# Expert stage of a perceiver block: SyncE's requests for page rows are tied to the landing of expert weights, and one request of ScalarE is moved

## The reference

```python
probs = sigmoid(x @ router_w.T + expert_bias)        # 160 experts
top_w, top_idx = top_k(probs, 8)
top_w = 2.5 * top_w / (sum(top_w) + 1e-9)
h1 = silu(einsum('th,eih->eti', x, w_gate))          # 256 -> 128 for each expert
routed = einsum('eti,ehi->th', h1 * combine.T, w_down)   # 128 -> 256
out = x + routed + silu(x @ w_gate_shared.T) @ w_down_shared.T
```

## Time and profile before

| | |
|---|---|
| median of 3 runs | 1392.87 us (1391.3 to 1392.95) |
| profiled execution, its time | 1392.75 us |
| its span, first to last instruction | 1391.3 us |
| TensorE busy | 1244.5 us (89%) |
| the steps of the expert stage | from 1012.9 us to 1328 us of the span |
| reading back and summing | from 1339 us to the end |

### The profile page before, as it was taken

How to read it: one execution, slowest core, us unless ns; L and a number is a source line. 1 busy time by engine, 2 the same in 40 slices (tenths; PEclk the granted TensorE clock), 3 DMA queues, 4 the chain that set the end, 5 groups by cost and what they waited for, 6 DMA issues and landing times. The chain is left out here.

```text
span 1391.3 us, 34815 instructions
## 1 busy us (share of the span) xinstructions
PE 1244.5 (89%) x11693; PEld 900.0 (65%) x11693; DVE 945.6 (68%) x2728; ACT 604.5 (43%) x1761; POOL 548.3 (39%) x717
## 2 busy tenths in 40 slices
PE   4999999999998589999999999997759999999946
PEld 2667667767766357777767677766537766766725
DVE  2477666666666446787788877877627776767737
ACT  2445555455454156676566676574201111111140
POOL 1011111101100102456566566667506766766730
PEclk8999999999999679999999999999959999999969
DMA  9322323233323000111121111113298988898658
GB/s 290 114 91 96 132 90 140 90 132 107 132 80 106 31 16 16 48 53 56 60 76 56 64 53 61 60 37 110 90 278 245 266 257 259 260 256 252 204 226 349
DMA packets 124881, 185.74 MB, mean 134 GB/s; under 512 B 23286, under 2 KB 90517, under 8 KB 122785
## 3 DMA queue, kind: packets, MB, share of 16 engines
q10 hardware_dynamic: 57696, 77.47, 17.7%
q1 hardware_dynamic: 50880, 71.38, 17.0%
q0 software_dynamic: 16128, 34.67, 7.0%
HBM read 190.88 MB, written 78.25 MB: 193 GB/s over the span
## 5 line engine op out<-in xcount | busy, mean ns | idle before, releaser
L1052 POOL DMA_INDIRECT y_d<-y,xg x208 | 203.7, 979 | 128.9 <-DVE y L1048 92.7
L1022 ACT ACTIVATE ex<-bank 128x256 f32<-128x256 f32 x104 | 39.9, 383 | 286.4 <-PE bank L1017 98.7
L773 POOL DMA_INDIRECT xs_d<-xw,slot_id x128 | 134.7, 1053 | 30.3 <-issue 29.4
L472 ACT ACTIVATE ex<-bank,nmC 128x256 f32<-128x256 f32 x256 | 118.9, 481 | 14.3 <-DVE nmC L466 13.8
L1048 DVE COPY y<-bank 128x512 f32<-128x512 f32 x104 | 71.8, 691 | 75.3 <-PE bank L1042 71.6
L485 PE MATMUL bank<-ident,ex 128*128 128x128 f32 x512 | 79.1, 284 | 19.9 <-ACT ex L472 16.5
L485 PEld LDWEIGHTS bank<-ident,ex 128*128 128x128 f32 x512 | 61.8, 145 | 54.3 <-ACT ex L472 21.0
L466 DVE TENSOR_REDUCE nmC<-bank 128x2 f32<-128x512 f32 x128 | 82.8, 680 | 5.6 <-PE bank L457 4.8
L1006 DVE COPY ex<-bank 128x512 f32<-128x512 f32 x104 | 71.4, 687 | 21.9 <-PE bank L1002 18.2
L1002 PE MATMUL bank<-ident,xg 128*128 128x128 f32 x416 | 70.7, 295 | 16.7 <-DMA xg<-xs_d 16.7
L1316 POOL TENSOR_TENSOR stB<-stB,small 128x1 f32<-128x1 f32 x32 | 20.2, 632 | 165.3 <-DVE stB L1313 165.3
(11 more groups left out here) (390 smaller groups left out, 3317.7 us busy)
## 6 DMA issues: line engine op xcount, KB each, us to landing
xs_d<-zeros ACTq DMA_DIRECT2D x16, 1768.0 KB, 7.4
pTC<-in_wexp ACTq DMA_DIRECT2D x104, 256.0 KB
xg<-xs_d SPq DMA_DIRECT2D x306, 68.0 KB
cT<-in_ctx SPq DMA_DIRECT2D x32, 512.0 KB, 4.1
wh<-in_wexp ACTq DMA_DIRECT2D x52, 256.0 KB
cT<-in_wexp ACTq DMA_DIRECT2D x52, 256.0 KB
kTC<-in_wexp ACTq DMA_DIRECT2D x52, 256.0 KB
vvC<-in_wexp ACTq DMA_DIRECT2D x52, 256.0 KB
```

Of the source, the lines that this page charges most:

```text
L472: last = act.activation(ex[:, u, 256 * b:256 * b + 256], bank[hp][:, 256 * b:256 * b + 256], ACT.Exp, bias=nm[:, u, b:b + 1], accum_out=su ...
L773: pool.indirect_dma_start(out=xs_d, out_offset=bass.IndirectOffsetOnAxis(ap=slot_id[z][:, k:k + 1], axis=0), in_=xw[z][:, k, :], in_offset ...
L1052: pool.indirect_dma_start(out=y_d, out_offset=bass.IndirectOffsetOnAxis(ap=who, axis=0), in_=y[:, n, g, :], in_offset=None, bounds_check=l ...
```

## The change

```
+    GATED = range(2, UNITS)
...
         def rows_sp(m):
+            if m in GATED:
+                d = 2 * (m - 2)
+                sp.wait_ge(s_w[d % RING_W], (d // RING_W + 1) * 64)
             page = load_numbers(nc, mybir.EngineType.SP, table[1], m, 4 if m < EARLY else 8)
             fetch(sp, 2 * m, page, range(4 if m < EARLY else 3))
...
         rows_act(0)
         load(0)
         load(1)
-        for m in range(1, EARLY):
-            rows_act(m)
+        rows_act(1)
         for m in range(UNITS):
             rows_sp(m)
         for i in range(DOUBLES + DOWN):
             if i < RING_W - 2:
                 load(i + 2)
             elif RING_W <= i + 1 < DOUBLES:
                 load(i + 1)
+            if i == 1:
+                rows_act(2)
             if i < DOUBLES:
                 turn(i)
```

## The result

Over 20 runs each the changed kernel takes 1397.76 us in the median and the kernel before 1394.33 us. The ratio is 1.0027, with a 95% interval of 1.0015 to 1.0040: slower by 3.8 us (2.1 to 5.6). The prediction was 1400 us against a median of 1392.87, so slower by 7.1 us, with the rows of the page requests landing last.

The account below looks back on a forecast made before the run. The prediction saw a DMA-bound start and a TensorE-bound long stretch. Its terms, -3 us at the start and +10 us steady, made +7 us: 1400 us, with an 8-in-10 range of 1388 to 1414.

Parts of the forecast that it names:

- What bounds the kernel: Whole expert stage: a start bound by DMAs, then a long stretch bound by TensorE at 2.69 us a step.
- Start, SyncE: -3 us: First eight steps: gates hold back row pages, so weights land sooner; 3 us gained, bounds 0 to 5.4 us.
- the 18 pages: Start: pages not yet requested when weights of double 5 land, 24 in place of 42; 1.25 MB or 4.3 us.
- Start, ScalarE: nothing: Start: loads 2 and 3 requested 3.2 us sooner, load(4) no sooner; no term in the sum.
- Steady stretch: +10 us: Long stretch: gated rows land last; 17 units lose 0.85 us in the mean, 15 us less a third; bounds 0 to 45.
- The room: Steady stretch: time from just-in-time weights at the gate to the `turn` that needs the rows, 4.6 us.
- rival A: Whole kernel: rows become the last to land, slower by 3 to 21 us, 1396 to 1414; chance 0.58.
- B: Gate hidden in the steady stretch and weights profit from held-back rows: faster, 1385 to 1390; chance 0.22.
- C: Both terms small or equal: start -3 us, steady loss 1 to 5 us, 1391 to 1395.7; chance 0.20.
- D: SyncE's gate does nothing because the ring's wait opens later than the gate; chance 0.
- The fit: Steady stretch: 2.0 us plus bytes at 436 GB/s; a page lands in 2.2 us, need 4.2 us, no stall, 1390.

Follow-up runs that it names:

- three gates with the move: Changed kernel with SyncE gates kept for units 2 to 4 alone and the moved ScalarE request: 1386.73 us, ratio 0.9955 to the kernel before.
- the move alone: Changed kernel without any gates, only ScalarE's four page requests of double 5 behind the weights of double 3: 1392.45 us, ratio 0.9995.
- late gates alone: Changed kernel with gates kept for units 8 to 51 alone and the moved ScalarE request: 1403.25 us, ratio 1.0058 to the kernel before.
- another place of the same gate: Changed kernel with the wait from unit 8 on put between requests for double 2m and double 2m + 1: 1390.30 us, ratio 0.9978.
- the tighter gate: Changed kernel with the gate from unit 8 on at weights of double 2m - 3 in place of 2m - 4: 1412.31 us, ratio 1.0123.
- a looser gate: Changed kernel with the gate from unit 8 on at weights of double 2m - 6 in place of 2m - 4: 1388.13 us, ratio 0.9973.

## Why the prediction was right

**What bounds the kernel.** Right for the kernel before. In its start TensorE waits for weights while the DMA engines are full, and its long stretch follows TensorE, with weights just in time. In the start of the changed kernel TensorE waits for no weights any more; the first Silu and the clock are what is left there besides the first rows.

**Start, SyncE: -3 us.** The mechanism was right, the size too small. When `up(5)` begins, SyncE has made 24 requests in the changed kernel and 42 in the kernel before, exactly the count of the prediction, and the waits for weights are gone. The profile shows -4.4 us; three gates with the move give 6.3 us in the timed runs. The 4.4 us agree with the 4.3 us that I had counted for the 18 pages before I took off what later units take back. That is luck in part: 2.5 us are the waits for weights, and some 1.4 us came from the clock, which the prediction left out. `up` of double 5 was to begin 2 to 5 us sooner; it began at 1046.81 with the stage 3.8 us later, so 4.4 us sooner against its stage.

**Start, ScalarE: nothing.** Right for the move alone, 0.9995. Load(2) and load(3) are issued 3.6 and 3.4 us sooner after step 0, as forecast, and load(4) and the first Silu are not. I had not seen that TensorE would wait 7.0 us for that Silu; having it sooner brought nothing in the timed runs. Beside the gates the traces give the move some 1.7 us, which the prediction put at nothing.

**Steady stretch: +10 us.** The need after the gate was put at 6.3 us and is 6.1 us in the unit shown; its parts are 0.53 us for the numbers, 3.98 us for the last landing, and 1.6 us mostly between them, for issuing the requests. The room of 4.6 us and the deficit of 1.7 us answer to a wait of 1.46 us in the row shown; 15 to 20 waits of 0.5 to 2 us were forecast and 18 came, the longest 2.3 us. The late gates alone cost 8.1 us. The two runs that gave the rows more room, by another gate or by another place of the same gate, took the loss away, and the one that took room away raised it. So the cause is shown. The count of SyncE's waits was off: 22 of them name weights, not 40; at the other gates the landing had been counted before SyncE came.

That the size of 10 us fits the measured 9.6 us is partly luck. The prediction had 15 us of waits for rows and took a third off, because a stall gives its neighbours time. The waits for rows are 16.4 us and nothing of this kind is seen to come off. What came off are 9.4 us of waits for weights, which the prediction expected to stay, and 2.1 us of busy time at the lower clock were added, which it didn't have.

The sum, -3 + 10 = +7, was 3 us above the measured +3.8: in the timed runs the gates at the start are worth 5.3 us and the late gates cost 8.1 us. The time of 1397.76 us lies in the lower part of rival A's range. The rule of the tighter gate, which I carried on from the same arithmetic, was too high by about three times, so the steady term's arithmetic holds near the point where it begins to bite and not far beyond.

**The rivals.** B, weights profit from quiet rows, failed in the long stretch. I had named falling weight waits as its sign, and they did fall, from 10.1 to 0.7 us; that sign was badly chosen. TensorE came later to them, and with a looser gate they were back. At the start B's mechanism is borne out. C, both terms small, is out: each is larger than C allows, and they partly cancel. D was rightly excluded.

The Trainium skill, "DMA: Bandwidth & Descriptors", section "Rules for kernel authors", says to issue early and wait late; the late gates' 8.1 us agree. The start is the exception that the rule doesn't speak of: there, with the DMA engines full (share 1.07), a request that is made early takes time from one that is needed sooner. On the same page, the Trainium skill's section "Issuing engines are not separate DMA queues" says that DMAs of all issuers interleave on the same engines, and the start agrees: with 24 requests of SyncE in place of 42, ScalarE's weights land before they are needed. The fit that the prediction took from this page of the Trainium skill, about 2.0 us plus bytes at 436 GB/s, stands there in the section "Anatomy of one DMA — SWDGE (gpsimd) path", for DMAs that GpSimd issues, while these requests are SyncE's. As an estimate it gives 2.2 us for one page of rows. The trace has 3.98 us for the last of three in this traffic, and with the fit's figure there would have been no loss.

## What to carry to other kernels

In this kernel a gate that holds back early transfers paid only where the DMA engines were the bound, and only for as long; find the stretch in the busy time by stretch and put the gate there. Before gating in steady state, measure two things in the trace: the time from the gating event to the need, and the whole way of a gated transfer from the gate to its landing, reading of numbers and issue included. And don't take a wait that disappears from the list for a cure: see whether another one stands in front of it, and compare the sums.

## What the runs showed of the hardware that was not expected

In the changed kernel the granted clock fell once in the long stretch. By stretch, from 1204 to 1214 us:

```profile
1204.00:1208.00 4.00, 1.66 (x21) 1.06 (x18) 2.84 (x11) 0.38 (x1) 2.75 (x4) 1.00 0.72 215
1208.00:1210.00 2.00, 2.00 (x24) 1.83 (x25) 1.02 (x2) 0.00 (x0) 0.98 (x1) 0.79 0.78 208
1210.00:1212.00 2.00, 2.00 (x11) 0.88 (x8) 0.09 (x1) 0.38 (x1) 0.00 (x0) 0.50 0.50 141
1212.00:1214.00 2.00, 2.00 (x24) 1.83 (x25) 1.97 (x7) 0.00 (x0) 0.98 (x1) 0.86 0.51 110
```

TensorE was busy for 1.66 of 4 us, with a wait of 2.35 us for rows, and then was granted 0.50 of its clock (1.2 GHz in place of 2.4) for some 3 us. The step from 1207.84 to 1211.80 us took 3.96 us in place of 2.69, so here 1.3 us were lost on top of the wait. In the kernel before, whose longest such wait was 1.4 us, the clock stayed at 1.00 all through the stretch. But the length of the wait doesn't decide it by itself. With gates on units 2 to 7 TensorE waited 2.75 us for rows, until 1051.02, and the clock stayed at 1.00:

```profile
1048.00:1050.00 2.00, 0.27 (x4) 0.00 (x0) 1.35 (x6) 0.38 (x1) 1.57 (x2) 1.00 1.08 294
1050.00:1052.00 2.00, 0.98 (x10) 0.81 (x12) 0.23 (x1) 0.00 (x0) 1.24 (x2) 1.00 1.04 350
```
